# An LSTM over 512 steps on one core: twelve plain steps in place of sixteen, the initial state cast by ScalarE, and other zero products at the start

## The reference

```
xW = einsum('ntd,dk->tnk', x, Wx) + b
def step(carry, xw_t):
    prev_h, prev_c = carry
    a = xw_t + prev_h @ Wh
    i, f, o = sigmoid of the first three quarters of a
    g = tanh of the last quarter
    next_c = f * prev_c + i * g
    next_h = o * tanh(next_c)
out = x + transpose(hs, (1, 0, 2))
```

## Time and profile before

| what | us |
|---|---|
| median of 3 executions | 2535.98 (2535.93 to 2538.73) |
| the profiled execution | 2535.94 |
| its span on the core | 2534.1 |
| PE busy | 2515.8 (99% of the span) |
| PE weight loads (beside PE) | 1795.3 (71%) |
| DVE busy | 1983.6 (78%) |
| ACT busy | 1247.9 (49%) |
| POOL busy | 7.2 |

### The profile page before, as it was taken

How to read it: one execution, slowest core, us unless ns; L and a number is a source line. 1 busy time by engine, 2 the same in 40 slices (tenths; PEclk the granted TensorE clock), 3 DMA queues, 4 the chain that set the end, 5 groups by cost and what they waited for, 6 DMA issues and landing times.

```text
span 2534.1 us, 155783 instructions
## 1 busy us (share of the span) xinstructions
PE 2515.8 (99%) x67134; PEld 1795.3 (71%) x67134; DVE 1983.6 (78%) x8602; ACT 1247.9 (49%) x5266; POOL 7.2 (0%) x12
## 2 busy tenths in 40 slices
PE   8999999999999999999999999999999999999998
PEld 3577777777777777777777777777777777777775
DVE  7877777777777777777777777777777777777776
ACT  6544444444444444444444444444444444444443
POOL 1000000000000000000000000000000000000000
PEclk9999999999999999999999999999999999999999
DMA  8101101101011011010110110101101001011000
GB/s 234 37 20 30 33 17 33 28 21 33 17 33 33 17 33 25 24 33 17 33 33 17 33 25 25 33 17 33 33 17 33 25 25 33 17 33 33 17 17 18
DMA packets 142169, 80.21 MB, mean 32 GB/s; under 512 B 8620, under 2 KB 139836, under 8 KB 141372
## 3 DMA queue, kind: packets, MB, share of 16 engines
q1 hardware_dynamic: 140548, 75.40, 11.3%
q0 software_dynamic: 1152, 4.19, 0.9%
q10 hardware_dynamic: 440, 0.20, 0.0%
HBM read 42.02 MB, written 33.55 MB: 30 GB/s over the span
## 4 chain that ended last, share of the span: by engine, by line
PE 98%; DVE 1%; DMA 0%; ACT 0%; issue 0%; SPq 0%; DVEq 0%
PE even L327 26%; PE odd L327 26%; PE odd L321 26%; PE even L321 13%; PE s1t_sum L321 6%; DMA w_raw<-in_L_cond_Wx_dram 0%; DVE hw_lo L796 0%; PE odd L340 0%; PE plain_odd L327 0%; PE even L340 0%; PE plain_even L327 0%; PE plain_odd L340 0%; PE plain_even L340 0%; DVE xw_lo L796 0%; DVE f_c L709 0%
## 5 line engine op out<-in xcount | busy, mean ns | idle before, releaser
L709 DVE TENSOR_TENSOR f_c<-i_f,c_state 128x64 f32<-128x64 f32 x1024 | 233.0, 228 | 449.1 <-ACT i_f L561 449.1
L561 ACT ACTIVATE i_f<-odd 128x128 f32<-128x128 f32 x504 | 145.3, 294 | 536.8 <-PE odd L327 536.8
L327 PE MATMUL even<-hw_hi,hT_hi 128*32 128x512 f16 x4032 | 392.1, 379 | 2.4 <-issue 1.9
L327 PE MATMUL odd<-hw_hi,hT_hi 128*32 128x512 f16 x4032 | 392.1, 379 | 1.5 <-DVE hT_hi L658 1.5
L327 PE MATMUL even<-hw_lo,hT_hi 128*32 128x512 f16 x4032 | 392.1, 379 | 0.0
L327 PE MATMUL odd<-hw_lo,hT_hi 128*32 128x512 f16 x4032 | 392.1, 379 | 0.0
L321 PE MATMUL odd<-xw_hi,xT_hi 128*32 128x256 f16 x7936 | 388.6, 273 | 0.0
L321 PE MATMUL odd<-xw_hi,xT_lo 128*32 128x256 f16 x7936 | 388.6, 273 | 0.0
L321 PE MATMUL odd<-xw_lo,xT_hi 128*32 128x256 f16 x7936 | 388.6, 273 | 0.0
L561 ACT ACTIVATE i_f<-even 128x128 f32<-128x128 f32 x504 | 145.3, 294 | 426.1 <-PE even L327 426.1
L571 ACT ACTIVATE tanh_c<-c_state 128x64 f32<-128x64 f32 x1024 | 279.4, 273 | 99.8 <-DVE c_state L719 41.1
(11 more groups left out here) (127 smaller groups left out, 4098.0 us busy)
## 6 DMA issues: line engine op xcount, KB each, us to landing
x_ring<-in_x_dram SPq DMA_DIRECT2D x252, 128.0 KB, 2.8
out_dram<-x_ring SPq DMA_DIRECT2D x252, 128.0 KB
w_raw<-w_raw POOLq DMA_DIRECT2D x8, 512.0 KB, 5.9
w_raw<-in_L_cond_Wx_dram SPq DMA_DIRECT2D x3, 1024.0 KB, 9.4
w_raw<-in_L_cond_Wh_dram SPq DMA_DIRECT2D x3, 1024.0 KB, 15.5
w_raw<-in_L_cond_Wx_dram SPq DMA_DIRECT2D x2, 512.0 KB, 4.5
w_raw<-in_L_cond_Wh_dram SPq DMA_DIRECT2D x2, 512.0 KB, 19.4
x_ring<-in_x_dram SPq DMA_DIRECT2D x6, 64.0 KB, 18.1
```

Of the source, the lines that this page charges most:

```text
L327: mm = nc.tensor.matmul(bank[j * N:(j + 1) * N, :], hT[:, k * N:(k + 1) * N], w[:, k, j, :], start=False, stop=False, skip_group_check=True)
L561: nc.scalar.activation(i_f_half, bank_half, ACT.Sigmoid, scale=UNSCALE).then_inc(if_ready[two], 1)
L709: nc.vector.tensor_tensor(half_of(f_c[:, :], two), half_of(i_f[:, P:2 * P], two), half_of(c_state[:, :], two), ALU.mult)
```

## The change

`PLAIN` goes from 16 to 12, `REST_AT` from steps 5 to 12 to steps 4 to 11, while `CAST_AT` and `NEGATE_AT` stay. `passes_done` gives 11 passes to each step. PE's wait for the lo part of x stands only ahead of the passes that read it; the hi passes wait for the cast. `cast_plain` of an even step waits for one transpose instead of two. The h0 cast and the scaled `h0_last` go from DVE to ACT, ahead of its casts of Wh. `keep_going` is called six times instead of three: once after the bias products, once ahead of the recurrent product of step 0, twice after each of its first two blocks, and no longer ahead of the last weight tile. ACT and DVE unroll 16 steps as before, PE now 12.

```diff
-PLAIN = 16
+PLAIN = 12
...
-REST_AT = ((5, 5), (6, 6), (7, 7), (8, 8), (9, 9), (10, 10), (11, 11), (12, 12))
+REST_AT = ((4, 4), (5, 5), (6, 6), (7, 7), (8, 8), (9, 9), (10, 10), (11, 11))
...
+UNROLLED = -(-PLAIN // CHUNK) * CHUNK
...
-    return min(34 * step // 3, PASSES * (PLAIN - AHEAD)) if step < 13 else PASSES * (PLAIN - AHEAD)
+    return min(11 * step, PASSES * (PLAIN - AHEAD)) if step < PLAIN - 3 else PASSES * (PLAIN - AHEAD)
...
                     if n % PASSES == 0 or n == first:
                         pe.wait_ge(plain_seeded, t + 1 - AHEAD)
+                        pe.wait_ge(xp_hi_ready, t + 1)
+                    if part == 2 and (k == 0 or n == first):
                         pe.wait_ge(xp_ready, t + 1)
...
                 plain_lo(1)
+                keep_going()
                 pe.wait_ge(hT_lo_ready, 1)
...
                     recur_add(bank, hT_hi, hw_lo, k)
-                    keep_going()
+                    if k < J - 2:
+                        keep_going()
+                        keep_going()
...
             spread_bias(0, 1).then_inc(bias_spread, 1)
+            keep_going()
             for t in range(PLAIN):
...
             def cast_plain(t):
-                act.wait_ge(x_blocks_ready, blocks_count(t // GROUP, 2))
+                act.wait_ge(x_blocks_ready, blocks_count(t // GROUP, 1 + t % 2))
...
+            act.wait_ge(h0_loaded, 16)
+            nc.scalar.activation(h_hi[:, :], h0_raw[:, :], ACT.Copy).then_inc(h_hi_ready[0], 1)
+            nc.scalar.activation(h0_last[:, :], h0_raw[:, :].rearrange("p (e k) -> p e k", k=J)[:, :, J - 1], ACT.Copy,
+                                 scale=WSCALE).then_inc(h0_last_ready, 1)
             for k in range(J):
                 split_h_hi(k)
-            for t in range(PLAIN):
+            for t in range(UNROLLED):
...
-            dve.wait_ge(h0_loaded, 16)
-            nc.vector.tensor_copy(h_hi[:, :], h0_raw[:, :]).then_inc(h_hi_ready[0], 1)
             transpose_h(h_hi_ready[0], h_hi, hT_hi, hT_hi_ready[0], 1)
...
-            nc.vector.tensor_scalar(out=h0_last[:, :], in0=h0_raw[:, :].rearrange("p (e k) -> p e k", k=J)[:, :, J - 1],
-                                    scalar1=WSCALE, scalar2=None, op0=ALU.mult).then_inc(h0_last_ready, 1)
```

More of the change, by code:

```diff
@@ L51 @@
 CAST_AT = (3, 4, 5, 6, 7, 8, 9, 10)
-REST_AT = ((5, 5), (6, 6), (7, 7), (8, 8), (9, 9), (10, 10), (11, 11), (12, 12))
+REST_AT = ((4, 4), (5, 5), (6, 6), (7, 7), (8, 8), (9, 9), (10, 10), (11, 11))
 BIAS_AT = 0
+UNROLLED = -(-PLAIN // CHUNK) * CHUNK
 AHEAD = 4
 PASSES = 12
-def passes_done(step):
-    return min(34 * step // 3, PASSES * (PLAIN - AHEAD)) if step < 13 else PASSES * (PLAIN - AHEAD)
 HALVED = (0, 7)
@@ L67, with passes_done @@
 F_EARLY, F_LATE = slice(0, 3), slice(4, 8)
+def passes_done(step):
+    return min(11 * step, PASSES * (PLAIN - AHEAD)) if step < PLAIN - 3 else PASSES * (PLAIN - AHEAD)
 def lstm_residual(nc, x, h0, w_x, w_h, bias, out):
@@ L646, in _ @@
                         cast_plain(t)
+            act.wait_ge(h0_loaded, 16)
+            nc.scalar.activation(h_hi[:, :], h0_raw[:, :], ACT.Copy).then_inc(h_hi_ready[0], 1)
+            nc.scalar.activation(h0_last[:, :], h0_raw[:, :].rearrange("p (e k) -> p e k", k=J)[:, :, J - 1], ACT.Copy,
+                                 scale=WSCALE).then_inc(h0_last_ready, 1)
             for k in range(J):
                 split_h_hi(k)
-            for t in range(PLAIN):
+            for t in range(UNROLLED):
                 step(t, t % CHUNK, CHUNK, t // CHUNK)
-            steps(mybir.EngineType.Activation, step, begin=PLAIN // CHUNK)
+            steps(mybir.EngineType.Activation, step, begin=UNROLLED // CHUNK)
         @block.vector
@@ L848, in _ @@
             dve.wait_ge(c_zeroed, 1)
-            for t in range(PLAIN):
+            for t in range(UNROLLED):
                 step(t, t % CHUNK, CHUNK, t // CHUNK)
-            steps(mybir.EngineType.DVE, step, begin=PLAIN // CHUNK)
+            steps(mybir.EngineType.DVE, step, begin=UNROLLED // CHUNK)
 _INS = ['x', 'cond_1024', 'L0_cond_Wx', 'L0_cond_Wh', 'L0_cond_b']
```

## The result

| what | before | after |
|---|---|---|
| median | 2536.31 (21 executions) | 2540.49 (21 executions, 2539.57 to 2541.73) |
| the profiled execution | 2535.94 | 2540.63 |
| its span | 2534.1 | 2538.8 |

The ratio is 1.0013, with a 95% interval of 1.0007 to 1.0019: slower by 4.2 us, 0.16%. That lies inside the range, in the class "within 0.2%" and on the side of the forecast, 1.7 times its size (4.2 against 2.45). By the ratio it is 3.3 us, between 1.8 and 4.8.

The account below looks back on a forecast made before the run. PE was taken to bound the kernel, with 98% of the chain of waits. Terms -0.59 - 1.20 + 0.35 + 3.89 gave +2.45 us on 2535.94, so 2538.4, range 2536.8 to 2540.9.

Parts of the forecast that it names:

- the largest term: PE's stall at the jump into the loop, step 12, waiting for the last piece of A22: +3.89 us.
- The case called most likely: The forecast of 2538.4 us, between 2537.6 and 2539.1, with no rival happening; chance 0.72.
- A: Rival: the clock falls to 1.2 GHz in the stall ahead of step 12, losing 1.2 to 2.2 us; 2540.1; chance 0.15.
- B: Rival: PE fetches the loop's code only after its release, up to 1.4 us instead of 0.25; 2539.5; chance 0.08.
- the signs that the prediction named: Behind the stall: passes about twice 0.216 us (A); PE's first row over 0.5 us after the piece's end (B).
- The price of the jump: PE's jump into the loop at step 12 with an empty queue: between 0 and 1.4 us, taken as 0.25.
- four places where PE waits: The start (held by DVE), step 1 (by ACT), step 14 (0.28 us for `hT_hi`) and the very end.
- The pairs: Four plain steps become two pairs, each pair 9.76 us where two plain steps took 10.36: 1.20 us less.
- The wait on S2: Step 10, the first `middle`, waits for the last piece of S2; `recur` of step 11 starts 0.35 us later.
- Eleven passes cover the chain: In plain steps PE needs 4.97 us with 11 passes, the chain 4.69; 0.28 us to spare, so nothing lost.
- The start: Moving the h0 cast (0.37) and the waits on x (0.22) bring `recur` of step 2 0.59 us earlier.
- The zeros: Dropping zero products ahead of the last weight tile and adding others while PE waits for DVE: taken as 0.

Follow-up runs that it names:

- wait_at_use: Changed kernel, but PE unrolls 16 steps and waits for the lo part of A22 only at the first product reading it, in step 12: 2533.03 us, ratio 0.9982.
- zeros_in_stall: Changed kernel with 16 passes of zeros into an unused bank just ahead of the wait for A22: 2537.06 us, ratio 0.9999.
- pad_after: Changed kernel with its six `keep_going` calls issued as 256-column matmuls, 144 more PE instructions ahead of the loop: 2539.96 us, ratio 1.0011.
- stall_no_jump: Changed kernel with PE unrolling 16 steps, the wait for A22 still ahead of step 12 but without the jump: 2538.45 us.
- rests_earlier: Changed kernel with its lo pieces dealt out earlier, S2 complete in step 8 and A22 in step 10, PE's program the same: 2533.57 us, ratio 0.9987.

## Why the prediction was right, and where it was off

The sign, the largest term and the range were right. The case called most likely, 2537.6 to 2539.1 without A or B, did not happen: by the signs that the prediction named, both A and B did, which it put above the range. Between the two profiles the sum of +2.45 was off by +1.13 (jump), +2.19 (clock), +0.14 (S2), +0.58 (start) and -1.92 (exit), which gives the +4.57. That the time still lay in the range is luck of the last term.

**The largest term had the right cause.** The wait for the last piece of A22 at the loop, behind `add_out` in DVE's queue, was forecast as a stall of 3.89 us. The piece ended 8.46 after `recur` of step 11 began (forecast: 8.49, from 102.80 to 111.29). wait_at_use, which moves only this wait and the jump, took 7.5 us away.

**The price of the jump was mis-sized.** The step "I take 0.25, this end of the range is the nearer one" failed: the gap was 1.46, the upper end of 1.4 and the 0.05 of an ordinary wait, which I had put as rival B at 0.08. The jump by itself is what I took it for: 0.34 and 0.35 from piece to first row with it (zeros_in_stall, pad_after), 0.06 without (stall_no_jump). The other 1.1 come with the place of the code (1.46 against 0.35 in pad_after). DVE's jump was no row for that.

**Rival A happened.** The clock fell in the stall and step 12 paid 2.19, at the upper end of the 1.2 to 2.2 that the start gave. Its chance of 0.15 was too low. The clock fell in a shorter idle too, 3.75 us in the profile of pad_after, and, by times and mean clocks, in most executions of stall_no_jump; in rests_earlier it fell behind a row of idles of at most 0.93. The case against it, one idle of 2 us without harm, did not reach that far. The Trainium skill ("TensorE: Matmul & The Clock Gate", Part 1) says that idleness returns the clock to 1.2 GHz: the trace agrees, 0.50 granted from about 89.8 on. Idleness at one stretch is not the whole of it: stall_no_jump kept the full clock through 3.45 us, and rests_earlier lost it without a long idle.

**The exit was not in the sum at all.** The prediction lists four places where PE waits, the last of them the very end; there, ahead of step 511, PE waits 1.25 us before and after. The list lacked a fifth. The row of 1.92 idle at 2512.48 stood in the profile before and I did not read it. The change moves PE's code, and the idle went. By chance it offset much of A and B: 5.02 - 3.89 = 1.13 and 2.19 too little, 1.92 too much.

**The pairs** gave the forecast 1.20, to within 0.01. **The wait on S2** cost 0.49 against 0.35: PE began S1 0.93 late (80.57 where 79.64 was free), 0.12 more than forecast, of which 0.07 are a transpose of x ahead of the piece that took 0.72 here, not 0.65. **Eleven passes cover the chain**: no idle in steps 2 to 9, not even with three halves in a step.

**The start** was sized about right and yet is not in the profile. DVE saves 17.26 to 20.52 against 16.50 to 20.25, 0.49 (forecast 0.37), and ACT's order 0.28 (forecast 0.22), from the first Wh rest to `recur` of step 2, 16.80 against 17.08. But ACT's last two casts of Wx began at 16.17, behind 1.38 us of waiting for the weights, where they began at 15.41 before, and that took the gain back; the forecast had no term for the arrival of the weights. The later arrivals are no fixed cost of the change, as stall_no_jump shows; the first rest of Wh moved between 19.47 and 21.62 from profile to profile.

**The zeros** ahead of the last tile were worth nothing, as forecast: PE waited for `hT_hi` of step 0 afterwards for 0.89 us instead of 0.38.

**What stays open:** what PE waits for at the loop's entry. That the gap depends on the place of the code is shown by pad_after; but no instruction transfer is under way in it. At the exit the transfer of the instructions fits by its time, which is more than a likely reading and less than proof. Nor was a profile taken in which the weights land early with the changed kernel's own code; pad_after, with the same start, has `recur` of step 2 at 36.27.

## What to carry to other kernels

When work is moved to fewer steps, look for the last wait on each piece and at what stands ahead of the producer in its queue; a wait placed ahead of a loop for convenience is free only while the piece is long done, and belongs at the first use. Price a stall of PE together with what follows it: here the restart at half clock cost 2.2 us and the gap behind the release 1.5 on top of 3.6, and zeros into an unused bank bought the 2.2 back. Before a few us are counted as gain or loss, read the rows without a releaser at loop entries and exits, since any edit can move them.
